# A new order of calls for the front and the last block of an attention and feed-forward kernel

## The reference

```python
q = silu(xn @ Wq1 @ Wq2);  f = sigmoid(xn @ Wk1 @ Wk2);  v = xn @ Wv      # xn = layernorm(x)
a = exp(log_sigmoid(f));   k = 1 - a
h[t] = a[t] * h[t-1] + k[t] * v[t]                                         # scan over the 512 tokens
out = rms_norm(q * h) * norm_w @ Wo
x = x + layernorm(out)
y = layernorm(x)
for i in range(6):
    y = gelu(y @ W1[i].T + B1[i]) @ W2[i].T + B2[i] + y
    if i < 5: y = layernorm(y) * LN_G[i] + LN_B[i]
x = x + layernorm(y)
```

## Time and profile before

| | |
|---|---|
| time, median of 3 runs | 627.94 us (627.71 to 628.29) |
| profiled execution | 629.86 us, of which span 628.0 us |
| granted TensorE clock, mean | 0.998 |
| PE busy | 619.8 us (99%), 2893 matmuls |
| DVE busy | 470.1 us (75%) |
| ACT busy | 407.9 us (65%) |
| POOL busy | 250.4 us (40%) |
| chain that ended last | PE 92%, DVE 3%, issue 2%, ACT 2%, POOL 1% |

### The profile page before, as it was taken

One profiled execution on the slowest core, in us unless ns is written; L12 is line 12 of the kernel. 1 busy time (PEld: TensorE's weight loads), 2 busy tenths in 40 slices (PEclk: granted clock), 3 DMA queues, 4 the chain that ended last, 5 costly groups with the idle time before them and its releaser, 6 DMA issues.

```text
span 628.0 us, 8878 instructions
## 1 busy us (share of the span) xinstructions
PE 619.8 (99%) x2893; PEld 516.4 (82%) x2893; DVE 470.1 (75%) x820; ACT 407.9 (65%) x688; POOL 250.4 (40%) x232
## 2 busy tenths in 40 slices
...
DMA packets 56877, 25.13 MB, mean 40 GB/s; under 512 B 47360, under 2 KB 52864, under 8 KB 56832
## 3 DMA queue, kind: packets, MB, share of 16 engines
...
## 4 chain that ended last, share of the span: by engine, by line
PE 92%; DVE 3%; issue 2%; ACT 2%; POOL 1%; POOLq 0%; DVEq 0%; ACTq 0%
PE BK L169 47%; PE BK L351 38%; PE BK L301 3%; PE BK L175 1%; PE BK L366 1%; PE BK L198 1%; DVE OL L534 1%; PE BK L242 0%; POOL X L1188 0%; ACT R L835 0%; PE BK L262 0%; PE BK L253 0%; PE BK L254 0%; PE BK L232 0%; ACT R L849 0%
## 5 line engine op out<-in xcount | busy, mean ns | idle before, releaser
L945 ACT ACTIVATE HH<-BK,B 128x512 fp32r<-128x512 f32 x192 | 132.1, 688 | 140.5 <-PE BK L169 136.2
L563 DVE TENSOR_TENSOR HL<-BK,HH 128x512 fp32r<-128x512 f32 x192 | 130.7, 683 | 83.3 <-ACT BK L951 82.8
L169 PE MATMUL BK<-XH,WL 128*128 128x512 f32 x416 | 162.5, 391 | 0.7 <-DVE HL L563 0.7
L169 PE MATMUL BK<-XL,WH 128*128 128x512 f32 x416 | 162.1, 390 | 0.0
L169 PE MATMUL BK<-XH,WH 128*128 128x512 f32 x416 | 162.0, 389 | 0.0
L351 PE MATMUL BK<-HH,WL 128*128 128x512 f32 x368 | 143.7, 390 | 0.0
L351 PE MATMUL BK<-HH,WH 128*128 128x512 f32 x368 | 143.2, 389 | 0.0
L351 PE MATMUL BK<-HL,WH 128*128 128x512 f32 x368 | 143.2, 389 | 0.0
L951 ACT ACTIVATE BK<-BK,B 128x512 f32<-128x512 f32 x192 | 125.8, 655 | 0.0
L169 PEld LDWEIGHTS BK<-XH,WL 128*128 128x128 f32 x416 | 78.1, 188 | 17.3 <-DVE HL L563 1.1
L169 PEld LDWEIGHTS BK<-XH,WH 128*128 128x128 f32 x416 | 78.1, 188 | 16.5
...
## 6 DMA issues: line engine op xcount, KB each, us to landing
...
sums<-P SPq DMA_DIRECT2D x40, 8.0 KB, 1.4
...
```

The lines of the kernel that those rows point to most:

```text
L169: r = eng.matmul(dst, s, m, start=i == 0, stop=i == len(todo) - 1)
L563: eng.tensor_tensor(HL[:, g % HR, :], bank["mm1", n, j][:, :], HH[:, g % HR, :].bitcast(f32), ALU.subtract).then_inc(S["hlo"], 1)
L945: eng.activation(HH[:, g % HR, :], bank["mm1", n, j][:, :], ACT.Gelu, bias=B1[:, 8 * (n // 4) + j:8 * (n // 4) + j + 1]).then_inc(S["ghi"], 1)
```

## The change

In five lists, the calls of the front and of the last block stand in another order. The loops between them, the body of every call and its waits stay as they are. No call is added or taken away. The lists of TensorE differ in the front alone (its last block is the same); SP's list differs in the last block alone. As the lists say little by themselves, a few lines of each are shown, and the rows of the instruction order stand below.

```diff
 # TensorE, the front
-            turn3(3, 1, 2); mm2(2, 1); mm1(2, 4, 3); mm2(2, 2); mm1(2, 5, 1); mm2(2, 3); mm1(2, 6, 2); mm2(2, 4)
-            mm1(2, 7, 0); mm1(3, 0, 3); mm2(2, 5); mm1(3, 1, 1); mm2(2, 6); mm1(3, 2, 2); mm2(2, 7); mm1(3, 3, 0)
...
+            mm2(1, 4); rms(3, 2); mm1(1, 7, 0); mm2(1, 5); mm2(1, 6); mm1(2, 0, 1); mm1(2, 1, 2); mm1(2, 2, 3)
+            mm1(2, 3, 0); mm2(1, 7); mm2(2, 0); mm2(2, 1); turn3(3, 0, 1); turn3(3, 1, 2); mm2(2, 2); mm1(2, 4, 3)
+            mm1(2, 5, 1); mm1(2, 6, 2); mm2(2, 3); mm1(2, 7, 0); mm2(2, 4); mm1(3, 0, 3); mm2(2, 5); mm1(3, 1, 1)
...
 # ScalarE, the front
-            ldx0(1); ldx0(3); warm(); wq1_hi(); wk1_hi(); first_xhi(0); wq2_hi(); first_xhi(1); wk2_hi(); uhi(0, 0)
+            ldx0(1); ldx0(3); wq1_hi(); warm(); first_xhi(0); wq2_hi(); first_xhi(1); wk1_hi(); wk2_hi(); uhi(0, 0)
...
-            l2_nm(3, 0); l2_nm(3, 1); l2_nm(3, 2); l2_nm(3, 3); ghi(2, 0); gf(2, 0); wp_hi(5); ghi(2, 1); gf(2, 1)
+            wp_hi(5); xn(3, 1); xhi3(3, 1); gf(2, 3); ghi(2, 4); ghi(2, 5); wp_hi(6); ghi(2, 6); gf(2, 4); gf(2, 5)
...
 # POOL, the front
-            mhalf(); quarter(); half(); idle_in(); eps(); f_ve(0); f_rs(0); f_ve(1); f_rs(1); wq2_lo(); wk2_lo()
+            idle_in(); mhalf(); f_ve(0); f_rs(0); quarter(); f_ve(1); f_rs(1); wq2_lo(); wk2_lo(); nw_minus(); eps()
...
-            l2_rs(3); l2_nb(3); x1(3, 0); x1(3, 1); x1(3, 2); x1(3, 3); l3_ng(3); l3_ve(3); l3_rs(3); wp_lo(5, 0)
-            l3_nb(3); wp_lo(5, 1); rsd(0); sum1(1); wp_lo(6, 0); wp_lo(6, 1); wp_lo(7, 0); wp_lo(7, 1); wp_lo(8, 0)
+            l2_nb(3); sum2(0); x1(3, 0); x1(3, 1); x1(3, 2); x1(3, 3); l3_ve(3); l3_ng(3); l3_rs(3); l3_nb(3); sum1(1)
+            wp_lo(5, 0); wp_lo(5, 1); rsd(0); wp_lo(6, 0); wp_lo(6, 1); sum2(1); wp_lo(7, 0); wp_lo(7, 1); wp_lo(8, 0)
...
 # VectorE, the last block
-            hlo(23, 7); fin0(2, 0); fin0(2, 1); fin0(2, 2); z_st(23, 0); z_st(23, 1); fin0(2, 3); z_mv(23, 0)
+            hlo(23, 7); fin0(2, 0); fin0(2, 1); z_st(23, 0); fin0(2, 2); z_mv(23, 0); z_st(23, 1); fin0(2, 3)
...
 # SP, the last block
-            stored(1, 3); away(2, 0); half_tokens(0); half_tokens(1); stored(2, 0); stored(2, 1); stored(2, 2)
+            tokens(1, 1); stored(0, 0); away(2, 0); stored(0, 1); stored(0, 2); half_tokens(1); half_tokens(0)
```

More of the change, by code:

```diff
@@ L378, in _ @@
[L378 to L387, removed]
@@ L716, in _ @@
[L716 to L720, removed]
@@ L726, in _ @@
[L726 to L730, removed]
@@ L731, in _ @@
[L731 to L733 removed]
+            one(); f_st(0); f_st(1); f_mv(0); f_mv(1); f_st(2); f_st(3); f_mv(2); f_mv(3); f_nm(0); f_nm(1); f_nm(2)
+            f_nm(3); wq1_lo(); first_xlo(0); first_xlo(1); wk1_lo(); ulo(0, 0); ulo(0, 1); l1_st(1, 0); l1_st(1, 1)
@@ new lines, in _ @@
+            l3_st(2, 3); l3_mv(2, 2); scan(3, 2); l3_mv(2, 3); tot1(0); o(3, 2); hlo(1, 3); olo(3, 1); kv(3, 3)
+            scan(3, 3); o(3, 3); olo(3, 2); hlo(1, 4); mub(0); ctr(0, 0); olo(3, 3); xlo3(2, 0); xlo3(2, 1)
+            sq_turn(3); sq_part(3); l2_st(3, 0); hlo(1, 5); l2_st(3, 1); l2_mv(3, 0); l2_st(3, 2); l2_mv(3, 1)
+            ms(3, 0); ms(3, 1); l2_st(3, 3); ms(3, 2); ms(3, 3); l2_mv(3, 2); l2_mv(3, 3); ctr(0, 1); hlo(1, 6)
+            tr2(0); hlo(1, 7); l3_st(3, 0); l3_mv(3, 0); l3_st(3, 1); l3_st(3, 2); l3_st(3, 3); l3_mv(3, 1)
```

198 lines of the change are left out of this document (106 added, 92 removed).

## The result

The changed kernel takes 639.52 us (median of 4 runs, 638.93 to 639.93), the kernel before in the same session 627.88 us. The ratio is 1.0184, 95% interval 1.0166 to 1.0201: slower by 11.6 us, above the whole stated range (625.2 to 629.6). The profiled execution took 638.93 us with a span of 637.1, 9.1 us more than the span of before. The rest of the 11.6 lies in which executions were traced: that of before was 2.0 us longer than its median, that of the changed kernel 0.6 shorter.

The account below looks back on a forecast made before the run. TensorE, busy for 99% at full clock, was taken as the bound, leaving only stalls, start and tail. The terms summed to -0.42 from 629.86 us profiled, 629.44; 1.92 lower for the median gave 627.5, range 625.2 to 629.6.

Parts of the forecast that it names:

- the loops between run close to the pace in both kernels: Between front and last block: TensorE's matmuls start near their pace before and after the change, so no term was given.
- tot1(1): VectorE waits for sums through DRAM ahead of `hlo(2, 5)`, stalling TensorE at `mm2(2, 5)`: +1.5 us, between 0 and +2.4.
- tot1(0): In tile 3's projections, VectorE waits 1.2 us for sums through DRAM, delaying TensorE's operands: +0.95, between 0 and +2.2.
- tile 3: Tile 3's projections: -0.65 for stalls that go, +0.95 for the wait on sums; net +0.3, from -0.65 to +1.55.
- The start's -0.12: POOL's memset of OH, for which TensorE's spin waits, now stands first: -0.12 us, 0 at the least.
- olo(0, 2): At `proj(0, 2)`, `olo(0, 2)` no longer runs beside POOL's `ssum(0, 1)`: -0.85 us, to 0 if a `wp_lo` meets it.
- proj(0, 1): In attention, `ohi(0, 1)` and `o(0, 1)` come earlier, so `olo(0, 1)` need not idle: -0.3 us, between -0.3 and 0.
- turn3(3): `l3_nb(3)` now stands ahead of the weights on POOL, ending TensorE's wait; with `mm2(1, 6)`: -0.8 us, to 0.
- The extra table load: ScalarE's start: moving `warm` behind `wq1_hi` needs one more table load, ahead of `first_xhi(0)`: 0, up to +0.2 us.
- The tail's: Last block: `z_st(23, 0)` and `z_mv(23, 0)` stand earlier, ahead of the last store: -0.25 us, from -0.3 to +0.5.
- The signs: Trace marks of being right: start about 1.29, `olo(0, *)` within 0.8, no `turn3(3)` wait, both `tot1` idle, `hlo` wait near 162.
- The slower rival: Both `tot1` waits on DRAM take VectorE, then TensorE, in full, and one `l3_nm` is late: 630.0 us, chance 0.21.

Follow-up runs that it names:

- nn2_late: Kernel before, with VectorE's `nn(2, *)` behind `tot1(3)`, `mub(3)`, `ctr(3, 0)`, `ctr(3, 1)` behind `hlo(5, 0)`, `xlo(2, *)` behind `hlo(5, 3)`: 628.38 us, ratio 0.9990.
- loop_fix: Changed kernel with VectorE's `tot1(1)`, `mub(1)`, `ctr(1, *)` back behind `hlo(2, 7)` and its statistics ahead of block-tile 6 put earlier: 631.21 us, ratio 1.0029 to before.
- last_only: Kernel before with only the last block's new lists of VectorE, ScalarE, GpSimd and SyncE: 629.67 us, ratio 1.0011.

## Why the prediction was wrong

*The step that failed* is the first one: "the loops between run close to the pace in both kernels", from which the beginning of the loop got no term. It cost 5.5 us of TensorE's lag. The prediction named a stall in the loops among what it might have missed, and did not price it. What the runs put in its place: at the end of the front the new list of VectorE puts `ctr(3, 1)` behind `nn(2, *)`, `red2(3)` behind `y(4, *)`, and `red1(4)` between `tot2(3)` and `vae(3)`. In the trace each step waits for the one before it. Counted from the start of `mm1(6, 0)`, VectorE is level with before at `tot1(3)`, 1.4 us later at `ctr(3, 1)`, 2.4 at `red2(3)`, 3.6 at `vae(3)`, and still 3.6 at `ctr(4, 1)`, of which some 1.2 are free. The way from `red2(3)` to `tot2(3)` is no part of it: 6.0 us, and 5.9 before. The first of these moves alone does not make it (nn2_late cost nothing); moved back together, the stall goes (loop_fix). Which of the other two it takes was not tested. The loop is not the only step that failed: without its 5.5 the rest of the table would still stand 3.5 above before, 631.4 us, where the range ended at 629.6.

*tot1(1)* had its mechanism right and its size wrong: +1.5 was forecast, 2.8 stood in TensorE's timeline, and taking the move back won 3 of lag. The forecast end of `tot1(1)`, "near 162", is 162.2 in the trace, by luck: `put1(1)` went out at 155.2 and not at 156, and from there to the start of `tot1(1)` were 6.7 us and not 5.9. `hlo(2, 5)` followed 0.6 us later than thought, and TensorE came to `mm2(2, 5)` at 161.3 and not at 162. The 5.9 is a misread row: beside the earlier trace rows no weight load was under way, the last had been issued 14 us earlier (at 312.76); what took 3.1 us there was the last of the four DMAs of `got2`. The row that has a load just ahead is `put1(8)` above, 3.56 us to `got1(8)` where 1.4 is usual. With that, the 4.7 of the earlier trace rows and the 0.7 that `put1(1)` stood behind `ldp(7)` on SyncE, the way is 7.5, as measured from the end of `red1(1)`.

*tot1(0)*: 1.2 us of idle time forecast, 1.30 measured; +0.95 for TensorE, and 0.85 at `proj(3, 1)`. Left out was the next step of the same chain: `olo(3, 2)` and `hlo(1, 4)` also moved back by it, +0.9 at `mm1(1, 5)`. What was to go went, -0.56 at `proj(3, 2)` and `proj(3, 3)` for -0.65. But `olo(3, 2)`, which the prediction took to be free of the `ssum` beside it, met one again (1.57 us, 1.74 before), and that is the other cause of the +0.9. So tile 3 stands at +1.7 instead of +0.3, and its range ended at +1.55.

*What held.* The start's -0.12 (the spin's first matmul at 1.29 instead of 1.41). The `olo(0, 2)` without `ssum` beside it: 0.69 us instead of 1.71, in the changed kernel at 27.71. Its -0.85 came as -0.9, the -0.3 of `proj(0, 1)` as -0.3, and the +0.1 of `turn3(0)` as +0.4: -0.87 for the stretch, where -1.05 was forecast. `turn3(3)` waits for no `l3_nm` any more. The extra table load cost nothing; ScalarE's start in the changed kernel:

```profile
5.01 0.42 ACT L794 ACTIVATE WH<-R 128x256 fp32r<-128x256 f32 x1 [2.07 <-DMA R<-in_wq]
5.44 1.28 ACT L782 ACT_TABLE_LOAD   x1
6.74 0.20 ACT L782 ACTIVATE WARM<-ONE 128x1 f32<-128x1 f32 x1
7.29 0.60 ACT L854 ACTIVATE XH<-BK 128x512 fp32r<-128x512 f32 x1 [0.35 <-PE BK L184]
```

From the end of the ACTIVATE ahead (5.43) to the start of the next (6.74) are 1.31 us, as in the earlier trace rows, and `first_xhi(0)` waited for TensorE alone. The 2.66 of the Trainium skill, page "ScalarE: Activation LUTs", section "What ACT_TABLE_LOAD costs", is not seen here either.

*The tail's* -0.25 did not come: last_only cost 0.86 us, with 0.29 at `mm2(21, 2)`, where `tot2(19)` stands ahead of `hlo(21, 2)`, the same fault a third time.

*The signs* that the prediction names as right all stand in the trace: the start at 1.29, no `olo(0, *)` above 0.7, no wait of `turn3(3)`, VectorE idle for 1.30 and 3.73 us at the two `tot1`, and TensorE's wait near 162. They watch the terms that were priced, and say nothing of the one that was not.

*The slower rival* had the mechanism (a wait for the sums takes VectorE and then TensorE) and two of the three places, and still ended at 630.0; the two waits cost 3.7 together, less than the 4.1 from which it was to decide. It counted each wait once, at its own place, and not what the lag does to the next link; and it had no term for a clock that falls after a gap.
